# The last tile's output in lots of 320 and 192 tokens in place of 256 and 256

## The reference, cut to what matters

```python
gate = x @ Wg + (x @ Ag[idx]) @ Bg[idx]        # 256 -> 1024, rank-16 part by the sample's adapter
up   = x @ Wu + (x @ Au[idx]) @ Bu[idx]
h    = silu(gate) * up
y    = h @ Wd + (h @ Ad[idx]) @ Bd[idx]        # 1024 -> 256
x    = x + (y @ (weight * scale[:, None]).T + bias)
```

## Time and profile before

| | us |
|---|---|
| median of 3 runs (lowest, highest) | 585.08 (584.74, 586.42) |
| the profiled execution's own time | 584.39 |
| its span, first to last instruction | 582.6 |
| PE busy | 567.7 (97%) |
| DVE busy | 370.9 (64%) |
| ACT busy | 242.6 (42%) |
| GpSimd (POOL) busy | 139.4 (24%) |
| granted TensorE clock, whole span | 1.00 |

### The profile page before, as it was taken

The page is one execution under the profiler, slowest core; times in us unless marked ns, Lnnn a source line. Parts: engine busy times, 40 slices in busy tenths (PEclk is TensorE's granted clock), DMA queues, the critical chain, the costliest instruction groups (busy, mean ns, idle before and its releaser), DMA issues.

```text
span 582.6 us, 10462 instructions
## 1 busy us (share of the span) xinstructions
PE 567.7 (97%) x3627; PEld 475.9 (82%) x3627; DVE 370.9 (64%) x906; ACT 242.6 (42%) x548; POOL 139.4 (24%) x121
## 2 busy tenths in 40 slices
PE   7888999999999999999999999999999999999996
PEld 5767999999999999978878778788788788787885
DVE  7898767656775567675584474665665645754734
ACT  2654567748756655553312323224134223123110
POOL 2002211747346343664011030030030030100000
PEclk9999999999999999999999999999999999999999
DMA  8995677874295231534014032041041050220012
GB/s 321 339 360 190 200 244 225 204 173 72 46 268 137 48 39 21 129 62 135 1 42 106 7 106 50 0 132 23 0 137 16 0 143 11 65 60 5 11 28 37
DMA packets 64799, 61.06 MB, mean 105 GB/s; under 512 B 37456, under 2 KB 56656, under 8 KB 63472
## 3 DMA queue, kind: packets, MB, share of 16 engines
q1 hardware_dynamic: 53312, 37.97, 21.5%
q0 software_dynamic: 9264, 22.22, 16.0%
q10 hardware_dynamic: 2176, 0.26, 0.3%
HBM read 45.17 MB, written 19.47 MB: 111 GB/s over the span
## 4 chain that ended last, share of the span: by engine, by line
PE 89%; DMA 5%; DVE 3%; SPq 2%; issue 0%; POOL 0%; ACT 0%; DVEq 0%
PE bank L1469 26%; PE bank L1470 25%; PE bank L1471 25%; PE bank L1784 5%; PE bank L1732 2%; DMA xT<-in_xT 2%; DMA x_sb<-in_x 1%; SPq L410 1%; DMA bdT<-in_bdT 1%; PE bank L1601 1%; PE bank L1724 1%; PE bank L1592 1%; PE bank L1751 1%; PE bank L1752 1%; PE bank L1829 1%; DMA xg<-flat_rows,slot_row 1%
## 5 line engine op out<-in xcount | busy, mean ns | idle before, releaser
L768 ACT ACTIVATE act<-bank 128x512 f32<-128x512 f32 x64 | 38.2, 599 | 182.8 <-PE bank L1784 182.8
L1425 DVE TENSOR_TENSOR prod<-bank,act 128x512 f32<-128x512 f32 x64 | 44.2, 690 | 97.5 <-PE bank L1784 97.2
L1274 DVE TENSOR_TENSOR hid_lo<-hf,hid_hi 128x512 fp32r<-128x512 f32 (+1 forms) x80 | 46.6, 585 | 51.2 <-ACT hf L689 50.7
L1469 PE MATMUL bank<-w_hi,hid_hi 128*128 128x256 f32 x256 | 71.7, 280 | 0.0
L1470 PE MATMUL bank<-w_lo,hid_hi 128*128 128x256 f32 x256 | 71.4, 279 | 0.0
L1471 PE MATMUL bank<-w_hi,hid_lo 128*128 128x256 f32 x256 | 71.3, 279 | 0.0
L686 ACT ACTIVATE hid_hi<-bank 128x512 fp32r<-128x512 f32 (+1 forms) x80 | 41.2, 515 | 64.6 <-PE bank L1471 63.2
L516 POOL DMA_INDIRECT x_rows<-y_sb,slot_row x32 | 52.9, 1654 | 42.8 <-ACT y_sb L656 27.5
L505 POOL DMA_INDIRECT xg<-flat_rows,slot_row x32 | 34.1, 1066 | 97.1 <-DVE slot_row L1120 48.9
L1469 PE MATMUL bank<-xs_hi,w_hi 128*128 128x512 f32 (+1 forms) x158 | 56.5, 357 | 0.0
L534 POOL DMA_INDIRECT b_pair<-b_rows,b_row x8 | 8.0, 1000 | 198.5 <-PE bank L1829 197.9
(11 more groups left out here) (328 smaller groups left out, 1270.2 us busy)
## 6 DMA issues: line engine op xcount, KB each, us to landing
w_raw<-in_L_ffn_W SPq DMA_DIRECT2D x8, 1024.0 KB, 6.9
flat_rows<-x_sb SPq DMA_DIRECT2D x8, 520.0 KB, 5.8
x_sb<-in_x SPq DMA_DIRECT2D x8, 512.0 KB, 8.6
x_rows<-in_x SPq DMA_DIRECT2D x4, 1024.0 KB, 8.4
outT<-out_sb SPq DMA_DIRECT2D x120, 32.0 KB
xT<-in_xT SPq DMA_DIRECT2D x3, 1024.0 KB, 7.8
xT<-in_xT SPq DMA_DIRECT2D x2, 512.0 KB, 10.9
wdT<-in_wdT SPq DMA_DIRECT2D x1, 1024.0 KB, 6.0
```

Source lines behind the costliest of these rows:

```text
L768: act.activation(act1[h % 2][:, :], bank[h % 2][:, :], ACT.Silu).then_inc(silu1, 1)
L1274: dve.tensor_tensor(lo[:, n], hf[s % 2][:, n], hi[:, n].bitcast(f32), ALU.subtract).then_inc(hid0, 1)
L1425: dve.tensor_tensor(prod[par][h][:, :], bank[2 + h % 2][:, :], act1[h % 2][:, :], ALU.mult).then_inc(prod1, 1)
L1469: pe.matmul(out, lh, rh, start=start, stop=False, skip_group_check=True)
```

## The change

Lot 0 has 320 tokens (10 samples), lot 1 has 192 (6 samples). Every matmul, mask, split and addition of the last tile's output follows these widths. On PE, chunk 5 of lot 0 moves from behind the low-rank product into step 7, ahead of it. The last DVE instruction has 64 columns in place of 128. Each queue stores 5 samples after lot 0, then 2, then 1, where it stored 4, 2 and 2.

```diff
+        LOTS = ((0, 320), (320, 192))
 def last_out(j, k):
-            return bank[7 - k if j else 4 + k][:, 0:BT // 2]
+            return bank[7 - k if j else 4 + k][:, 0:LOTS[j][1]]
 def last_stores(queue, side):
-            t, n = NB1 - 1, SB // 8
-            mine = [[8 * j + 4 * a + 2 * side + i for a in range(2) for i in range(n)] for j in range(2)]
...
-            for j in range(2):
-                for i, s_ in zip(mine[j], to[j]):
-                    if i % 8 == 2 * side:
-                        queue.wait_ge(out_ev, KD * (NB1 + j))
-                    elif j and i % 4 == 2 * side:
-                        queue.wait_ge(out_ev, KD * (NB1 + j) + 1)
+            t = NB1 - 1
+            lots = ([2 * i + side for i in range(5)], [10 + 2 * i + side for i in range(2)], [14 + side])
...
+            for j, lot in enumerate(lots):
+                queue.wait_ge(out_ev, KD * NB1 + (0, KD, KD + 1)[j])
+                for i, s_ in zip(lot, to[j]):
                     queue.dma_start(out_v[:, :, bass.ds(s_, 1), :], out_sb[1][:, :, i * 32:(i + 1) * 32].unsqueeze(2)
                                     ).then_inc(out_done[1], 16)
 def finish_last_v():
-                for j in range(2):
-                    c = slice(j * BT // 2, (j + 1) * BT // 2)
-                    masked(vm, bank[0], NB1 - 1, at_=j * SB // 2, n=SB // 2).then_inc(v_ev, 1)
+                for j, (at_, n) in enumerate(LOTS):
+                    c = slice(at_, at_ + n)
+                    masked(vm, bank[0], NB1 - 1, at_=at_ // 32, n=n // 32).then_inc(v_ev, 1)
 def finish_last(wait_store):
-                        for at_, n in ((0, P), (P, P)) if j and k else ((0, BT // 2),):
-                            to = slice(j * BT // 2 + at_, j * BT // 2 + at_ + n)
+                        for at_, n in ((0, P), (P, LOTS[1][1] - P)) if j and k else ((0, LOTS[j][1]),):
+                            to = slice(LOTS[j][0] + at_, LOTS[j][0] + at_ + n)
 def down_last(h, j, ks=range(KD)):    # and finish_last(j, k) on PE alike
-                s, c = KH * (NB1 - 1) + h, slice(j * BT // 2, (j + 1) * BT // 2)
+                s, c = KH * (NB1 - 1) + h, slice(LOTS[j][0], LOTS[j][0] + LOTS[j][1])
 def steps1(t, par, pair, first, last):
-                        for j in range(2) if h < KH - 1 else ():
+                        for j in range(2 if h < KH - 1 else 1):
                             down_last(h - 2, j)
...
-            for h in range(KH - 3, KH):
+            for h in range(KH - 2, KH):
                 down_last(h, 0)
```

More of the change, by code:

```diff
@@ L382, in last_stores @@
         def last_stores(queue, side):
-            t, n = NB1 - 1, SB // 8
-            mine = [[8 * j + 4 * a + 2 * side + i for a in range(2) for i in range(n)] for j in range(2)]
-            to = [[queue.value_load(sample_at[0:1, t * SB + i:t * SB + i + 1], min_val=0, max_val=TOK // 32 - 1) for i in half]
-                  for half in mine]
-            for j in range(2):
-                for i, s_ in zip(mine[j], to[j]):
-                    if i % 8 == 2 * side:
-                        queue.wait_ge(out_ev, KD * (NB1 + j))
-                    elif j and i % 4 == 2 * side:
-                        queue.wait_ge(out_ev, KD * (NB1 + j) + 1)
+            t = NB1 - 1
+            lots = ([2 * i + side for i in range(5)], [10 + 2 * i + side for i in range(2)], [14 + side])
+            to = [[queue.value_load(sample_at[0:1, t * SB + i:t * SB + i + 1], min_val=0, max_val=TOK // 32 - 1) for i in lot]
+                  for lot in lots]
+            for j, lot in enumerate(lots):
+                queue.wait_ge(out_ev, KD * NB1 + (0, KD, KD + 1)[j])
+                for i, s_ in zip(lot, to[j]):
                     queue.dma_start(out_v[:, :, bass.ds(s_, 1), :], out_sb[1][:, :, i * 32:(i + 1) * 32].unsqueeze(2)
@@ L1812, in finish_last @@
             def finish_last(j, k):
-                par, c = 1, slice(j * BT // 2, (j + 1) * BT // 2)
+                par, c = 1, slice(LOTS[j][0], LOTS[j][0] + LOTS[j][1])
                 pe.wait_ge(v_lo, NB1 + j)
```

## The result

The changed kernel is slower by a little: 586.91 us against 586.13 for the kernel before (medians of 22 runs each), ratio 1.0017, 95% interval 1.001 to 1.0024. By the ratio that is +1.0 us (0.6 to 1.4), where the sum said +0.94; the two medians themselves lie 0.78 apart.

A forecast was written before the change was run, and what follows sets the result against it. PE, busy 97% of the span, sets the computation's end, then DVE's last additions and stores given out follow. Later stores less the removed standstill give +0.94 us on 585.08, so 586.0 us, range 584.7 to 587.1.

The forecast's parts named there:

- (a): PE, steps 2 to 6 of the last tile: 30 pairs of 320- and 192-column products cost +0.59 us, all on the path.
- (b): PE, chunk 5 of lot 0 ahead of the low-rank product: that product 0.88 us later, nothing in the sum.
- (c): DVE masks and splits behind the low-rank product: slack before the first addition falls from 0.41 us to about 0.07, hidden barely.
- (d): End of wider lot 0: later on PE and longer DVE additions, so stores begin 1.28 us later.
- (e): Store queues: eight stores on each with no standstill, the last given out +0.94 us later.
- rival 1: PE: products cost by the line, 0.0932 us for 192 columns; end moves +0.35, to 585.4 us; chance 0.10.
- (f): Register loads, queue waits and transfers at the stores: unchanged in cost, nothing.
- Rival 2: PE: a narrow product costs as much as one of 256, 0.120 us; end +1.15, 586.2 us; chance 0.15.
- Rival 3: PE: smaller fixed part per product, 0.139 us at 320 and 0.086 at 192; end -0.28, 584.8 us; chance 0.07.
- Rival 4: PE, lot 1's 54 products: 192 columns fall to plain fp32's rate, 0.353 us; end about +13.5, 598.6; chance 0.13.

The follow-up runs named there:

- wide steps: 512-column products for chunks 0 to 4 in steps 2 to 6: changed kernel 1.0007, kernel before 1.000 (again 0.9991), each against the kernel before.
- the order alone: Kernel before (lots 256 and 256) with only chunk 5 of lot 0 moved ahead of the low-rank product: ratio 1.000 to the kernel before.
- 384 and 128: Changed kernel with lots of 384 and 128 tokens, stores 6, 1, 1 on each queue: ratio 1.0046 to the kernel before.

## Why the prediction was right or wrong

The sum was right, part by part, counted from the mark:

| step | foreseen | measured |
|---|---|---|
| 192-column product | 0.113 | 0.112 |
| 320-column product | 0.1466 | 0.146 |
| (a) steps 2 to 6 on PE | +0.59 | +0.57 |
| (a), (b) low-rank product starts later by | 1.47 | 1.44 |
| (c) slack left to DVE | 0.07 | 0.10 |
| (d) stores begin | +1.28 | +1.27 |
| (e) last store given out | +0.94 | +0.89 |
| all landed | +0.94 | +0.92 |

(In the table (a) is the low-rank product's 1.44 less the 0.87 of the six products that were moved ahead of it.) No term was off by more than 0.05 us, so the sum was not right by errors that cancel. (a) is the larger part of the loss, and the experiments show it from two sides: with wide steps in both, the new lots cost 0.32 us where they cost 0.89, so that 0.57 is (a), and making the lot narrower still (128) leaves its spacing where it is. The other 0.32 is (d) against the standstill: lot 0 is ready 0.70 later for its width alone, and only 0.38 of standstill was to be had. The prediction had this too, as rival 1's +0.35: even with products by the line the change could not win. (b) is shown by the order alone. (c) held barely, as said; the order alone shows what it costs without cover, 0.21 us that a standstill absorbed. (d) and (e), the end as the later of two sums, gave the last store of seven further kernels with two queues, to within 0.3 us for 384 and 128 and within 0.11 us for the other six. (f), the transfers, is unchanged: they landed 1.66 to 1.77 us after the last store was given out in all kernels with two queues (the prediction's 1.2 us for it was too short, but the same on both sides of its difference).

The prediction's line, 0.0131 + 0.000417 per column, is drawn through two spacings of before, 0.120 at 256 columns and 0.227 at 512. Between these widths the runs stay near it: 0.132 at 288 columns (line 0.133), 0.146 at 320 (0.1466), 0.175 at 384 (0.173). Below 256 they don't: 0.112 at 224, 192 and 128 (0.1065, 0.0932, 0.0665). Each of these products, whatever its width, has a weight load of 128x128 that takes 0.19 us in its trace.

**What was wrong** is the step from the sum to the outcome: "About 0.3% (1.8 us) is what a measurement of this kernel can tell from no change, so this is 'the same'". No row gives these 1.8 us; the nearest number is the scatter of three single runs, 1.7 us. But the interval of the ratio over 22 runs a side is 0.07% to each side, and 0.94 us is 0.16%: 1.0017 (1.001 to 1.0024) lies clear of 1, and the second comparison says the same with 1.0013 (1.0004 to 1.0022). It should have been called slower, and the chance of 0.80 on "the same" put a sum that I held likely (0.68) on the wrong side of what was measured. The absolute time was off for another cause: 586.0 came from a median of 585.08 over three runs, and the kernel before itself had medians of 586.13, 584.4, 586.68 and 584.44 in the four comparisons. The two comparisons of the changed kernel, at 586.13 and at 584.44, gave nearly the same ratio, so such a shift belongs in the range and not in the difference.

Rival 1 (products by the line) falls by the spacings of 192 and 128 columns. Rival 2 (no saving at all by narrowness) falls by less: 0.112 against its 0.120, and a last store 0.89 later against its 1.15. Rival 3 falls by 320 columns at 0.146. Rival 4 (plain fp32's rate, 0.353 at 192 columns) falls by the same rows: what it calls one pass is seen in the traces as one instruction for a product, and at 192 and at 128 columns it still is one, each 0.112 after the one ahead, where plain fp32 takes two for a product.

## What to carry to other kernels

Find the width below which a product gets no cheaper, and split its columns only into parts above it: here 224, 192 and 128 columns all cost 0.112 us and 256 cost 0.112 to 0.120. The narrower part saved 0.008 us at most, while the wider one cost 0.026 more at 320 columns, and the loss multiplies with every product of the accumulation, not only with those at the end. When stores at the end go by lots, write the end as the later of (first lot ready + all stores) and (last lot ready + its stores), and move the split only if both fall: a standstill on a queue isn't worth anything in itself (here 0.38 us of it went for a begin 0.36 later). And before calling a small difference "the same", compare it with the interval that many runs will give, not with the scatter of a few. Count from a mark that the change can't touch, for two profiled executions can differ by more before the mark than the change makes behind it (here 1.36 us against 0.92).

## What was not expected of the hardware

- fp32r products of 224, 192 and 128 columns have one and the same spacing, 0.112 us, in steady rows.
- With stores on GpSimd's queue at the end of the program, its closing DRAIN of 6.4 us ends 4.2 us beyond the landing of all stores (590.9 against 586.7); in the kernel before, a DRAIN of 11.7 us stands at 505.0, where no engine waits for it. The queue also started 1.23 us after SP's on the same addition.
- A last-tile product of 256 columns takes 0.120 us where the same form in layer 0 took 0.1125 at its quickest; why was not looked into.
